# The quarter-order copy of the normalised rows, moved from GpSimd to ScalarE

## The reference

```python
xn = _layernorm(x, axis=-1)
# branch 1: projection, a scan over the sequence, projection, bias
d = sigmoid(decay)
projected = einsum('bsd,ed->bse', xn, W_in)
state = d * state + (1.0 - d) * seg_t          # for each of the 512 steps
out1 = einsum('bsd,ed->bse', states, W_out) + bias
# branch 2: mixture of 32 experts, 6 a token, and a shared expert
scores = softmax(x2d @ wg_router.T);  topk_w, topk_idx = top_k(scores, 6)
ye = (silu(xe @ w_gate) * (xe @ w_up)) @ w_down   # xe: rows gathered by expert
out2 = weighted sum of ye + silu(x2d @ ws_gate) * (x2d @ ws_up) @ ws_down
x = x + out1 + out2
```

## Time and profile before

| | us |
|---|---|
| median of 3 runs | 983.61 (982.26 to 983.88) |
| the profiled execution, its own time | 971.35 |
| its span, first to last instruction | 969.5 |
| busy: TensorE, VectorE, ScalarE, GpSimd | 931.3, 647.4, 496.7, 510.2 |

### The profile page before, as it was taken

How to read it: one execution, slowest core, us unless ns; L and a number is a source line. 1 busy time by engine, 2 the same in 40 slices (tenths; PEclk the granted TensorE clock), 3 DMA queues, 4 the chain that set the end, 5 groups by cost and what they waited for, 6 DMA issues and landing times.

```text
span 969.5 us, 14039 instructions
## 1 busy us (share of the span) xinstructions
PE 931.3 (96%) x4596; PEld 838.0 (86%) x4596; DVE 647.4 (67%) x1098; ACT 496.7 (51%) x852; POOL 510.2 (53%) x375
## 2 busy tenths in 40 slices
PE   6899989999999999999999999999999999999992
PEld 6798978888888789899999999999989999999991
DVE  6778996454533676877667766776676677677640
ACT  5442324222222455765566656676566666566641
POOL 6210067777731425666666666566645645646341
PEclk9799999999999999999999999999999999999997
DMA  9406246030333569999899998999899999999842
GB/s 340 159 1 217 90 147 204 5 88 1 88 98 101 146 193 294 246 226 223 223 252 246 221 229 225 246 249 227 227 288 220 232 292 220 241 283 242 209 56 37
DMA packets 125834, 182.59 MB, mean 188 GB/s; under 512 B 19012, under 2 KB 72900, under 8 KB 125760
## 3 DMA queue, kind: packets, MB, share of 16 engines
q1 hardware_dynamic: 97840, 126.14, 41.5%
q0 software_dynamic: 26704, 55.01, 28.2%
q10 hardware_dynamic: 1216, 0.53, 0.2%
HBM read 114.21 MB, written 40.85 MB: 160 GB/s over the span
## 4 chain that ended last, share of the span: by engine, by line
PE 70%; DVE 9%; DMA 7%; issue 4%; SPq 4%; POOL 3%; ACT 2%; ACTq 1%; POOLq 0%; DVEq 0%
PE p_gu L967 12%; PE p_gu L968 12%; PE p_gu L969 12%; PE p_y L967 7%; PE p_y L968 7%; PE p_y L969 7%; SPq L379 4%; DMA xnT<-xn_rows,ids 4%; DMA xnT<-xnT 3%; PE p_gu L1051 2%; PE p_gu L1049 2%; DVE w_lo L1220 2%; POOL out L621 1%; PE p_y L953 1%; POOL xnT L607 1%
## 5 line engine op out<-in xcount | busy, mean ns | idle before, releaser
L621 POOL DMA_INDIRECT out<-rows,ids x112 | 201.8, 1802 | 220.8 <-ACT rows L680 196.4
L967 PE MATMUL p_gu<-xT_hi,w_hi 128*128 128x512 f32 (+12 forms) x816 | 286.8, 351 | 0.9 <-DVE xT_lo L1220 0.9
L969 PE MATMUL p_gu<-xT_hi,w_lo 128*128 128x512 f32 (+12 forms) x816 | 286.8, 351 | 0.0
L968 PE MATMUL p_gu<-xT_lo,w_hi 128*128 128x512 f32 (+12 forms) x816 | 286.7, 351 | 0.0
L607 POOL DMA_INDIRECT xnT<-xn_rows,ids x112 | 165.0, 1473 | 88.9 <-issue 33.3
L967 PEld LDWEIGHTS p_gu<-xT_hi,w_hi 128*128 128x128 f32 x816 | 155.2, 190 | 12.3 <-DVE xT_lo L1220 1.3
L968 PEld LDWEIGHTS p_gu<-xT_lo,w_hi 128*128 128x128 f32 x816 | 155.3, 190 | 10.9
L1220 DVE TENSOR_TENSOR w_lo<-raw,w_hi 128x1024 fp32r<-128x1024 f32 (+2 forms) x134 | 161.2, 1204 | 0.5 <-ACT w_hi L680 0.5
L969 PEld LDWEIGHTS p_gu<-xT_hi,w_lo 128*128 128x128 f32 x816 | 155.2, 190 | 7.2
L967 PE MATMUL p_y<-w_hi,hT_hi 128*128 128x512 f32 (+1 forms) x384 | 151.0, 393 | 3.8 <-DVE hT_lo L1220 2.0
L968 PE MATMUL p_y<-w_lo,hT_hi 128*128 128x512 f32 (+1 forms) x384 | 150.5, 392 | 0.0
(11 more groups left out here) (189 smaller groups left out, 1176.1 us busy)
## 6 DMA issues: line engine op xcount, KB each, us to landing
raw<-L_ffn_w_gate SPq DMA_DIRECT2D x32, 704.0 KB, 6.1
raw<-L_ffn_w_up SPq DMA_DIRECT2D x32, 704.0 KB, 8.1
xnT<-xnT SPq DMA_DIRECT2D x424, 48.0 KB
raw<-L_ffn_w_down SPq DMA_DIRECT2D x32, 512.0 KB
out<-rows SPq DMA_DIRECT2D x28, 256.0 KB, 3.1
xring<-L_attn_x SPq DMA_DIRECT2D x24, 256.0 KB, 3.9
raw<-L_ffn_w_down SPq DMA_DIRECT2D x32, 192.0 KB
xnT<-xnT SPq DMA_DIRECT2D x80, 64.0 KB
```

Of the source, the lines that this page charges most:

```text
L621: pool.indirect_dma_start(out=out[:, :], in_=y_sb[t][0:n, :], in_offset=None, out_offset=bass.IndirectOffsetOnAxis(ap=ids[0:n, col:col + 1 ...
L967: t_.matmul(dst, stat[0], mov[0], start=first, stop=False)
L968: t_.matmul(dst, stat[0], mov[1], start=False, stop=False)
L969: return t_.matmul(dst, stat[1], mov[0], start=False, stop=last)
```

## The change

The 16 copies are taken out of GpSimd's program, and ScalarE makes them, in pairs of tiles, through `reorder`. Source, destination, access patterns, waits and the semaphore that is raised stay as they were. GpSimd keeps the two transfers of zero rows that stood behind its fourth copy. Nothing changes in the programs of TensorE, VectorE and SyncE.

```diff
-            for t in range(TILES):
-                if t == 4:
-                    pool.wait_ge(s_nat[1], 16)
-                    for dst in (xn_rows, out):
-                        pool.dma_start(...).then_inc(s_zero, 16)
-                pool.wait_ge(s_xn, t + 1)
-                if t >= 4:
-                    pool.wait_ge(s_xns[t % 4], 16 * (t // 4))
-                g.tensor_copy(by_quarter[:, t % 4, :].rearrange("p (a s i) -> p a s i", a=QUARTERS, s=DC),
-                              rows[:, t % 4, :].rearrange("p (a i s) -> p a s i", a=QUARTERS, s=DC)
-                              ).then_inc(s_byq, 1)
+            pool.wait_ge(s_nat[1], 16)
+            for dst in (xn_rows, out):
+                pool.dma_start(...).then_inc(s_zero, 16)
...
+            def reorder(t):
+                for t in (t, t + 1):
+                    act.wait_ge(s_xn, t + 1)
+                    if t >= 4:
+                        act.wait_ge(s_xns[t % 4], 16 * (t // 4))
+                    copy(by_quarter[:, t % 4, :].rearrange("p (a s i) -> p a s i", a=QUARTERS, s=DC),
+                         rows[:, t % 4, :].rearrange("p (a i s) -> p a s i", a=QUARTERS, s=DC)
+                         ).then_inc(s_byq, 1)
...
             wT_hi(0, 3)
+            reorder(0)
+            reorder(2)
             normalise(4)
             normalise(6)
...
                 q(b, [1])
+                reorder(4 * b + 4)
                 normalise(4 * b + 8)
                 q(b, [2])
+                reorder(4 * b + 6)
                 normalise(4 * b + 10)
                 q(b, [3])
...
             xb_hi(2)
+            reorder(12)
+            reorder(14)
             act.wait_ge(s_lgm, 1)
```

More of the change, by code:

```diff
@@ L545, in _ @@
             g.memset(reset.rearrange("p (e i) -> p e i", i=TILES)[:, :, 0:1], 0.0).then_inc(s_reset, 1)
-            for t in range(TILES):
-                if t == 4:
-                    pool.wait_ge(s_nat[1], 16)
-                    for dst in (xn_rows, out):
-                        pool.dma_start(dst[T:ROWS, :].rearrange("(a p) d -> p a d", p=P),
-                                       zrow.unsqueeze(1).to_broadcast([P, 4, D])).then_inc(s_zero, 16)
-                pool.wait_ge(s_xn, t + 1)
-                if t >= 4:
-                    pool.wait_ge(s_xns[t % 4], 16 * (t // 4))
-                g.tensor_copy(by_quarter[:, t % 4, :].rearrange("p (a s i) -> p a s i", a=QUARTERS, s=DC),
-                              rows[:, t % 4, :].rearrange("p (a i s) -> p a s i", a=QUARTERS, s=DC)
-                              ).then_inc(s_byq, 1)
+            pool.wait_ge(s_nat[1], 16)
+            for dst in (xn_rows, out):
+                pool.dma_start(dst[T:ROWS, :].rearrange("(a p) d -> p a d", p=P),
+                               zrow.unsqueeze(1).to_broadcast([P, 4, D])).then_inc(s_zero, 16)
             pool.wait_ge(s_pre, 64)
```

## The result

The changed kernel took 1003.0 us as the median of 4 executions (994.56 to 1017.91), the kernel before 983.75 us on the same occasion (4 executions, 982.26 to 1000.21). The ratio is 1.0205, with a 95% interval from 1.0146 to 1.0264: slower by about 2%. The distance of 19.3 us is nearly twice the 10.4 that were forecast, and the time lies above the forecast (994.0) and above its range (989.5 to 1000.5). The direction and the place were right, the size was not. One thing must be known to read the times: single executions of one kernel lie up to 30 us apart, so a ratio with its interval counts only the executions within 1.5% of the fastest of their kernel, while a median counts all.

What follows compares the result with a forecast made beforehand. Everything waits for the first stage's last logits and `out_proj(0)`; late loads put these 9.9 us later, the clock adds 0.5, so 983.61 + 10.4 = 994.0 us, range 989.5 to 1000.5.

Steps and rivals of the forecast that it cites:

- What bounds the kernel, and where a delay goes: First stage: everything later waits for the last logits and `out_proj(0)` at 69.16 us; what moves this point moves the end.
- The path of the four loads: Loads of tiles 9, 11, 13, 15 wait behind stores needing ScalarE's copies: statistics late by 1.1, 5.7, 7.3, 11.6 us.
- From the last aggregate to `out_proj(0)`: Scan, factors, normalised tiles, evacuations and last logits take 10.0 us, before 11.6; the last logits end 9.9 us late.
- I take 0.55 with 0.62, as the only rows of this engine: ScalarE's 128x512 copy, priced from its copies without a step: 0.55 us each, 0.62 until the last one's result.
- Rival (1): ScalarE's copies take 1.12 us each, as on GpSimd: sum 13.6 us, 997.2 us in all; chance 0.17.
- The clock's term, 0.5 us: TensorE's idling drops one pair of transposes to the lower clock: 1.0 us a pair, taken half, 0.5 us.
- The base of 983.61 us: Median of the kernel before, to which 10.4 us was added; its profiled execution took 971.35, 12 us less.
- (2), landing late: Load of tile 9 takes 5.0 us again behind the zero rows: sum 12.3 us, 995.9 us; chance 0.08.
- (3), faster: No load comes too late, and VectorE's freed scans and factor row give back 3.86 us: 979.8 us; chance 0.04.
- (4), swallowed: First-stage delays are swallowed, no change: chance 0.03; partly swallowed, with 4 to 7 us left: 0.06.
- both dearer cases: Slow ScalarE copies together with late-landing loads: 15.7 + 0.5 = 16.2 us, 999.8 us, near the range's upper end.

Runs made afterwards that it cites:

- pair with few sends: The kernel before and the changed kernel, both with 16 of GpSimd's 96 sends (80 left out): medians 971.34 and 989.54 us.
- long copy: Changed kernel with 16 of 96 sends, ScalarE's copy still read with a step of 4, against the kernel before with 16 sends: 989.54 against 971.34 us.
- short one: Changed kernel with 16 of 96 sends, ScalarE's copy read without a step, against the kernel before with 16 sends: 982.01 against 971.34 us.
- few sends and timely loads: With 16 of 96 sends: the kernel before, twice (971.51, 971.34 us), and the changed kernel with SyncE's loads ahead of its stores (971.07 us).
- quiet base: The kernel before with 16 of GpSimd's 96 sends, the other 80 left out: median 971.34 us.

## Why the prediction was wrong, step by step

**What bounds the kernel, and where a delay goes: right.** The first stage's delay passed on in full. In the pair with few sends 18.15 us at the first base tile are 18.5 in the span. Two terms of the sum were too small, the copy's price and the clock. Together they missed 7.8 of these 18.2 us.

**The path of the four loads: right.** Each load stood behind a store that waited for ScalarE; VectorE's statistics waited for them. With the copy at the price that was assumed, the four loads and the four aggregates came within 0.9 us of the forecast, and the median time within 0.3 (10.7 against 10.4), the latter in part by chance. From the last aggregate to `out_proj(0)` the forecast had 10.0 us, and at full clock it was 10.1 (72.73 to 82.85 in the first profile).

**"I take 0.55 with 0.62, as the only rows of this engine": this step failed.** The copy takes 1.135 us, and that put the last aggregate 3.7 us later (15.3 against 11.6). Rival (1) had this price and a sum of 13.6; in the first profile `out_proj(0)` is 13.7 late, but the first base tile only 12.1. It was given a chance of 0.17, against which the prediction held that "they are other engines". This step alone would not have spoiled the forecast: 997.2 us lies inside the range. Two rows of other engines with a step, and the Trainium skill's rule on lines of 16 bytes (SBUF — State Buffer, "SBUF: two separate sides"), pointed to the upper end; one row without a step pointed to the lower. With and without the step ScalarE took 1.135 and 0.620 us, which agrees with the rule; no run tried another step.

**The clock's term, 0.5 us: this step failed too, and it is the larger part.** In the pair with few sends the other 4.1 us of the 7.8 stand behind the last aggregate, where TensorE ran at the low level. The forecast counted on 1.7 us less than before there and added 0.5; the profile has 2.9 us more than before. It took 1.0 us for one pair of transposes and halved it, and left out that the low level can hold on through the last logits (6.87 us in place of 3.66) and into `out_proj(0)`. In the profile it held from 78.64 to 91.5 us, and the first base tile is 6.4 us later than in the first profile of the changed kernel. The mean clocks put such a stretch into ten of twelve executions with the long copy and into one of seven with the short one, and into none of the eighteen executions with few sends and timely loads. So it goes with the late loads, and part of the 7.5 us between the medians of the long and the short copy (989.54 and 982.01) is the clock's. Why one execution gets it and the next does not stays open: just before it TensorE had waited only 1.07 and 0.33 us, and in the first profile, without it, 0.90 and 0.34.

**The base of 983.61 us: too few executions.** The medians of the kernel before on the later occasions were 992.16, 988.56, 996.81 and 992.76, so both first medians rest on four executions or fewer of a kernel that scatters more than the effect. The forecast saw the 12 us between the profiled execution and the median and passed over them with "if they hold for both kernels". The distance is what carries: 10.4 forecast, 18.2 measured on the quiet base, 19.3 between the first medians, whose closeness to 18.2 is partly luck.

**The rivals.** (1) was right in its price and its direct delay. (2), landing late, did not occur: the first two of the late loads took 3.63 and 3.04 us, near the 3.1 assumed. (3), faster, did not occur: even with all loads on time the kernel gained 0.3 us, not 3.86. (4), swallowed, did not occur. The upper end of the range had a slip: 9.9 us with both dearer cases (3.2 and 1.9) make 15.0, not 15.7; the measured time lies above either.

## What to carry to other kernels

When work is moved to another engine, look at what stands behind its semaphore in the DMA queue: here a load that had nothing to do with the copy stood behind its store, and that order, with the low clock behind it, cost 18 us, while the copies themselves cost no more than the freed scans gave back. For the price of a moved access pattern a row of another engine with the same pattern (1.12 us) was here the better guide to 1.135 than a row of the right engine with another (0.62). And before two profiles are compared, run the unchanged kernel several times: one execution without the usual pauses made this change look two to three times as dear as it is. A term for the clock should be priced over all the matmuls that can run at the low level, not over the first few.

## What the runs showed of the hardware

- ScalarE reads f32 from SBUF with a step of 4 elements in 1.135 us per 128x512, without a step in 0.620.
- A VectorE scan started during a pair of GpSimd's copies ends 1.08 to 1.09 us after that pair (five scans in the first profile of before, 1.61 to 2.04 us in place of 1.22). ScalarE's copies do not stretch it: 1.19 to 1.23 us.
- GpSimd's 96 indirect sends of 8-byte entries come, in eight of nine profiles, with pauses of TensorE, about 0.9 to 2.3 us each, that no wait of the program explains. They lengthen the part behind the first stage by 7 to 31 us. In five profiles with 16 sends there are none, and the executions of the kernel before lie within 6.4 us of one another instead of 24.4 on the same chip. What couples the two was not found.
- TensorE's granted clock was 0.50 after waits of 3.51 us (from 32.11 to 35.1 in the kernel before) and 4.42 us (from 66.09 to 70.9 in the changed one). But it was also 0.50 for 13 us from 78.64 on, behind waits of 1.07 and 0.33 us, and for 5 us in the first pass of `in_proj(1)`, which stands in the kernel before right behind 48 logits matmuls, without any wait (0.63 us a matmul from 43.06 on). Whether the long stretch came differed between executions of one program.
